# A two-layer transformer tower on one core: row maxima moved into their own layer's units, the stretch between iterations reordered, six heads' output projection moved into the attention

## The reference

```python
h = x @ W + pe                                            # 29 -> 128 channels
h = h + attn0(ln(h))      # group norm, 8 heads of 64, softmax over 1024 keys, wo, + its own input
h = h + ffn0(ln(h))       # tril(W1), gelu, tril(W2) over the 128 channels
h = h + attn1(ln(h))      # 8 heads of 16, softmax over 1024 keys, Wo
h = h + switch(ln(h))     # 16 experts, top 1, capacity 1.2, scaled by the route's probability
```

## Time and profile before

| | |
|---|---|
| median of 3 runs | 8374.74 us (8361.47 to 8421.3) |
| profiled execution, its own time | 8371.84 us |
| its span, first to last instruction | 8370.1 us |
| mean granted TensorE clock | 0.833 of full speed |
| busy PE / DVE / ACT / POOL | 88% / 60% / 38% / 21% |

### The profile page before, as it was taken

The page is one execution under the profiler, slowest core; times in us unless marked ns, Lnnn a source line. Parts: engine busy times, 40 slices in busy tenths (PEclk is TensorE's granted clock), DMA queues, the critical chain, the costliest instruction groups (busy, mean ns, idle before and its releaser), DMA issues.

```text
span 8370.1 us, 124378 instructions
## 1 busy us (share of the span) xinstructions
PE 7405.4 (88%) x39399; PEld 4297.5 (51%) x39399; DVE 5002.4 (60%) x11545; ACT 3213.9 (38%) x6291; POOL 1774.3 (21%) x1623
## 2 busy tenths in 40 slices
PE   6798998989989899898988989899898998989987
PEld 4555555545545455454555545555554555545532
DVE  5664665656666565565656656566565665656554
ACT  3343443433434343343433434334343443434431
POOL 2322222222222222222221222222222221222200
PEclk8887897988988878798887888879788787888866
DMA  2220211111121110211102111111111111111000
GB/s 63 47 47 20 49 32 40 39 43 36 26 49 39 33 39 23 49 39 33 39 22 52 37 43 39 29 43 29 43 39 41 31 32 43 38 40 39 22 24 7
DMA packets 89184, 308.91 MB, mean 37 GB/s; under 512 B 23942, under 2 KB 30022, under 8 KB 78278
## 3 DMA queue, kind: packets, MB, share of 16 engines
q1 hardware_dynamic: 88518, 300.53, 15.6%
HBM read 49.33 MB, written 41.94 MB: 11 GB/s over the span
## 4 chain that ended last, share of the span: by engine, by line
issue 63%; POOL 17%; PE 14%; DVE 4%; DMA 1%; POOLq 0%; SPq 0%; ACT 0%; DVEq 0%; ACTq 0%
POOL pr_lo L456 9%; POOL on L1183 3%; PE bank L776 3%; PE bank L749 2%; POOL on L1175 2%; PE bank L735 2%; PE bank L792 1%; PE bank L806 1%; PE bank L793 1%; PE bank L774 1%; DVE hm L1448 1%; DMA stacks<-parts 1%; DVE mxh L1458 1%; POOL h L1153 1%; PE bank L816 1%
## 5 line engine op out<-in xcount | busy, mean ns | idle before, releaser
L1458 DVE TENSOR_REDUCE mxh<-bank 128x1 f32<-128x512 f32 x4096 | 2761.3, 689 | 2300.8 <-PE bank L749 2275.4
L1029 ACT ACTIVATE pr<-bank 128x512 f32<-128x512 f32 x4096 | 2400.1, 598 | 3343.0 <-PE bank L776 3276.2
L749 PE MATMUL bank<-stacks 128*128 128x512 f32 (+1 forms) x4096 | 2036.1, 508 | 403.3 <-DVE mxh L1458 369.6
L776 PE MATMUL bank<-stacks 65*128 65x512 f32 (+1 forms) x4096 | 1929.2, 482 | 5.7 <-ACT pr L1029 5.7
L749 PEld LDWEIGHTS bank<-stacks 128*128 128x128 f32 (+1 forms) x4096 | 862.8, 214 | 1088.0 <-DVE mxh L1458 791.0
L456 POOL TENSOR_TENSOR pr_lo<-pr 128x1024 bf16<-128x1024 f32 x496 | 940.1, 1895 | 1933.7 <-ACT pr L1029 1933.7
L792 PE MATMUL bank<-v,pr 128*128 128x129 bf16 x8192 | 1308.1, 251 | 7.5 <-DVE pr_lo L456 5.1
L793 PE MATMUL bank<-v,pr_lo 128*128 128x129 bf16 x7936 | 1272.2, 251 | 0.0
L776 PEld LDWEIGHTS bank<-stacks 65*128 65x128 f32 (+1 forms) x4096 | 839.5, 210 | 767.7 <-issue 609.6
L774 PE MATMUL bank<-stacks 128*128 128x512 f32 x2048 | 1049.8, 513 | 47.0 <-issue 40.8
L792 PEld LDWEIGHTS bank<-v,pr 128*128 128x128 bf16 x8192 | 904.1, 113 | 357.1 <-issue 338.7
(11 more groups left out here) (180 smaller groups left out, 5209.8 us busy)
## 6 DMA issues: line engine op xcount, KB each, us to landing
stacks<-parts SPq DMA_DIRECT2D x384, 512.0 KB, 6.7
parts_d<-pr SPq DMA_DIRECT2D x16, 2048.0 KB, 6.5
stacks<-parts_d SPq DMA_DIRECT2D x224, 128.0 KB
stacks<-parts_d SPq DMA_DIRECT2D x224, 64.0 KB
stacks<-mrow SPq DMA_DIRECT2D x512, 2.0 KB
out<-hm SPq DMA_DIRECT2D x16, 512.0 KB, 2.7
stacks<-pr SPq DMA_DIRECT2D x32, 128.0 KB
stacks<-pr SPq DMA_DIRECT2D x32, 64.0 KB
```

The costliest lines, as they stand in the source:

```text
L749: mm(maxb[k % 2][:, :], qs[:, t * P:(t + 1) * P], ks[:, g * HALF:(g + 1) * HALF], start=True, stop=True).then_inc(max_filled.sem, 1)
L776: mm(bank[:, :], k_stack(layer, head)[0:last, kk], q_stack(layer, head)[0:last, q], start=(layer == 1), stop=True).then_inc(score_filled.s ...
L1029: act.activation(pr[:, at % 2, kt, :], score[k % 2][:, :], ACT.Exp, scale=SCALES[layer]).then_inc(exp_done.sem, 1)
L1458: dve.tensor_reduce(mxh[:, layer, n // 2, n % 2:n % 2 + 1], maxb[k % 2][:, :], AX_X, ALU.max)\
```

## The change

1. `tile_step` and `row_step` are shifted by two steps. A layer 0 unit's eight steps now hold only layer 0's tiles and a layer 1 unit's only layer 1's; before, the steps 6 and 7 of each unit held tiles of the other layer. Early tiles fall from 18 to 16.
2. `values1` is one piece of eight matmuls at step 3.
3. The expert blocks stand at s = 8m+5 of other units: seven layer 0 units (m = 12, 14, 20, 22, 24, 26, 28) and nine layer 1 units. Before there were four and twelve. Projections stand one slot earlier.
4. The output projection of heads 0 to 5 (`attn0a`) runs at the slots 244 and 247 of the attention; DVE adds it to `h0`. `serial` keeps the last two heads'.
5. `serial` has another order on every engine: layer norm 1 is applied before the old image's attention result is added; the first feed-forward matmul comes ahead of the next image's turn; the next image's group norm and heads come ahead of layer norm 2; POOL's two residual sums come last; the early maxima of layer 0 stand between two halves of the next image's values.

```diff
     if layer == 0:
-        return n - 18 if n < 8 else n - 10
-    return n - 10 if n < 8 else n - 2
+        return n - 16 if n < 8 else n - 8
+    return n - 8 if n < 8 else n
...
-    return (((-8, 8), (0, 16))[layer] if kind in BOTH else (-4, 4))[g]
+    return (((-6, 10), (2, 18))[layer] if kind in BOTH else (-4, 4))[g]
...
+def partial_slots(kind):
+
+    return {"first": {"attn0a.0": 113, "attn0a.1": 118}, "final": {}}.get(kind, {"attn0a.0": 244, "attn0a.1": 247})
...
-        first = [8 * m + 2 for m in sorted([*range(7, 31, 2), 14, 18, 22, 26])]
+        first = [8 * m + 5 for m in (7, 11, 12, 13, 14, 15, 19, 20, 21, 22, 23, 24, 26, 27, 28, 29)]
...
+                for g in range(2):
+                    yield partial_slots(seg.kind)[f"attn0a.{g}"]
+                    heads_out(seg, f"attn0a.{g}", g, range(NCH - 1))
...
-            def values1(seg, at, j):
+            def values1(seg, at):
                 _, u = units_of(seg.kind)[at]
                 n = o_place(seg.kind, 1, u)
-                te.wait_ge(exp_done.sem, exp_done.at(seg, 8 * at + 4 * j + 4))
-                if j == 0:
-                    te.wait_ge(o_drained.sem, o_drained.at(seg, n - 1))
+                te.wait_ge(exp_done.sem, exp_done.at(seg, 8 * at + 8))
+                te.wait_ge(o_drained.sem, o_drained.at(seg, n - 1))
```

In `serial`, on DVE:

```diff
+                if seg.l0:
+                    norm_apply(seg.l0, 1, h)
+                if seg.nxt:
+                    await_drained(dve, seg, "h0", "h1")
+                    norm_stats(seg, 0, h0)
                 if seg.l1:
                     dve.wait_ge(hm_copied.sem, hm_copied.at(seg.l1, 1))
                     for g in range(2):
                         add_result(seg, f"attn1.{g}", g, hm, hm)
...
+                if seg.nxt:
+                    embed_var(seg, "")
+                    embed_norm(seg, seg.nxt)
+                    embed_heads(seg, "", seg.nxt)
+                if seg.l0:
                     await_drained(dve, seg, "ffn_o0", "ffn_o1")
                     norm_stats(seg, 2, h)
```

In `serial`, on POOL:

```diff
                 if seg.nxt:
+                    rstd(seg, seg.nxt, 4)
+                if seg.l0:
+                    rstd(seg, seg.l0, 2)
+                if seg.nxt:
                     residual0(seg, seg.nxt)
-                if seg.l0:
-                    rstd(seg, seg.l0, 2)
-                if seg.nxt:
-                    rstd(seg, seg.nxt, 4)
```

More of the change, by code:

```diff
@@ L176, in glue_plan @@
     for name in SERIAL_NAMES:
-        wanted = kind != "first" if name in OLD_NAMES else kind not in ("penult", "final") if name in EMBED_NAMES \
+        after = next_kind(kind)
+        wanted = after is not None and int(name[1]) in layers_of(after) and early_row(after, int(name[1])) if name[0] == "M" \
+            else kind != "first" if name in OLD_NAMES else kind not in ("penult", "final") if name in EMBED_NAMES \
             else kind != "final"
         uses += [name] if wanted else []
-    after = next_kind(kind)
-    for layer in layers_of(after) if after else ():
-        uses += [f"M{layer}.0.0"] if early_row(after, layer) else []
     if kind == "final":
@@ L689, in done_heads, with heads_out @@
                         heads_turn(seg, c, g)
+                for g in range(2):
+                    yield partial_slots(seg.kind)[f"attn0a.{g}"]
+                    heads_out(seg, f"attn0a.{g}", g, range(NCH - 1))
+            def heads_out(seg, name, g, chunks):
+                bank, filled = use(seg, name, *(f"oT0.{c}.{g}" for c in chunks))
+                for j in range(4):
+                    t = 4 * g + j
+                    for c in chunks:
+                        last = mm(bank[:, j * P:(j + 1) * P], heads_T(c)[:, t * P:(t + 1) * P], wo_sb[:, c, :],
+                                  start=(c == chunks[0]), stop=(c == chunks[-1]))
+                last.then_inc(filled, 1)
             def old_turn(seg):
@@ L841, in serial @@
                 at = len(units_of(seg.kind)) - 1
-                for j in range(4 if seg.kind == "first" else 2):
-                    values(seg, at, j)
+                after = next_kind(seg.kind)
+                for j in range(4):
+                    if seg.kind == "first" or j < 2:
+                        values(seg, at, j)
                 if seg.l0:
@@ L852, in serial @@
                     for g in range(2):
[L853 to L859 removed]
+                        heads_out(seg, f"attn0.{g}", g, (3,))
                 if seg.nxt:
@@ L875, in serial @@
                 if seg.nxt:
+                    for g in range(2):
+                        z_turn(seg, seg.nxt, 0, g)
                     embed_group(seg, "", seg.nxt, 0)
@@ L902, in serial @@
                 if seg.nxt:
-                    embed_values(seg, "")
+                    embed_values(seg, "", range(4))
+                    early(seg, "next", after, 0)
+                    embed_values(seg, "", range(4, T))
                 if seg.l0:
-                    early(seg, "next", next_kind(seg.kind))
-                if seg.l0:
+                    early(seg, "next", after, 1)
                     await_drained(te, seg, "v1.0", "v1.1")
@@ L925, in segment @@
                     embed_values(seg, "a.")
-                    early(seg, "now", "first")
+                    early(seg, "now", "first", 0)
                     await_drained(te, seg, "a.v0.6", "a.v0.7")
@@ L1098, in serial @@
                 if seg.nxt:
-                    embed_values(seg, "")
-                after = next_kind(seg.kind)
-                for layer in layers_of(after) if after else ():
-                    if early_row(after, layer):
-                        max_rows(seg, f"M{layer}.0.0", seg.following(layer), layer, 0, 0)
+                    embed_values(seg, "", range(4))
+                    max_rows(seg, "M0.0.0", seg.nxt, 0, 0, 0)
+                    embed_values(seg, "", range(4, T))
+                if seg.l0 and early_row(after, 1):
+                    max_rows(seg, "M1.0.0", seg.l0, 1, 0, 0)
             def segment(seg):
@@ L1228, in serial @@
                 if seg.nxt:
[L1229 removed]
+                    residual0(seg, seg.nxt)
             def segment(seg):
@@ L1562, in serial @@
                 if seg.nxt:
-                    embed_values(seg, "", seg.nxt)
+                    embed_values(seg, "", seg.nxt, range(4))
+                    early(seg, "next", after, 0)
+                    embed_values(seg, "", seg.nxt, range(4, T))
                 if seg.l0:
-                    early(seg, "next", next_kind(seg.kind))
+                    early(seg, "next", after, 1)
             def segment(seg):
@@ L1578, in segment @@
                     embed_values(seg, "a.", seg.l0)
-                    early(seg, "now", "first")
-                beside = [Beside(more_heads(seg))] if seg.l0 else []
+                    early(seg, "now", "first", 0)
+                beside = [Beside(more_heads(seg)), Beside(partial(seg))] if seg.l0 else []
                 if seg.sw:
```

105 lines of the change are left out of this document (46 added, 59 removed).

## The result

The changed kernel takes **9098.2 us** (median of 4 runs, 9088.7 to 9128.4), the kernel before 8382.4 in the same measurement: ratio **1.085**, 95% interval 1.081 to 1.090. The forecast was 8420, its range ended at 8620. Slower was the side with the largest chance (0.36), but the size lies far outside. The profiled execution lasts 9086.9 us, 716.8 more than before.

The account below looks back on a forecast made before the run. Attention bound by PE's work in layer 0 units and a three-engine chain starting layer 1. Terms -16 + 18 + 3 + 4 - 4 = +5, times 14 is +70, second segment -20: 8371.8 + 50 = 8422, forecast 8420 us, range 8190 to 8620.

Parts of the forecast that it names:

- the blocks' places: Expert blocks in the attention: matmul cost plus stalls rise from 44 to 62 us, +18 an iteration, bounds 0 and +26.
- The stalls: Multiply-adds ahead of the low half lengthen seven layer 1 starts by 2.1 us; ahead of max tiles, nine stalls of 2.1.
- 6.3 was asked for: Sign of being right: layer 0 units with a block take 6.3 us or more from last score to first values, not 4.27.
- The clock: PE clock falls at layer 1 starts (2.2 us each) and new layer 0 stalls: +3 an iteration, bounds -20 and +14.
- after a wait of 0.69 in weak work: Argument for the slower rival: at the start of layer 1 the clock now falls after PE waits 0.69 us.
- The second rival: Multiply-adds ahead of layer 0 units' first tiles drop the clock in all nine places: +24 an iteration, about 8690, chance 0.23.
- Tiles and values1, -16 an iteration: In attention units, own-layer tiles and one-piece values1 save 1.2 us a pair over 13 pairs: -16, bounds -8 and -20.
- a bound of -8: Smallest saving from tiles and values1 in the attention, if DVE is late wherever PE is early: -8 us an iteration.
- Six heads, +4: 48 projection matmuls return on PE in the last pair, 2.7 us at each of two slots, partly covering a wait: +4.
- Serial, -4: Serial stretch: layer 1's q comes 2 us earlier, early tiles save 0.8, one collision costs 1.9: -4, bounds -10 and +2.
- The collision: In serial, POOL's residual sums start as DVE applies layer norm 2: eight operations take 4.07, not 2.14; one stop, +1.9.

Follow-up runs that it names:

- The added matmuls: Changed kernel with two more block-size matmuls, results unread, at steps 2 and 3 of layer 1 units of pairs 6, 10, 12, 14: 8975.9 us, ratio 1.070.
- the early matmuls: Changed kernel with the blocks' matmuls on PE at 8m + 2 and 8m + 3, multiply-adds on DVE left at step 7: 8977.4 us, ratio 1.067.
- the run with the wait: Changed kernel with old places of blocks and projections, and POOL's two residual sums held until layer norm 2 is applied: 8318.9 us, ratio 0.993.
- 8247: Kernel before with values1 in one piece, six heads in the attention, and POOL's layer norm 1 sum held until the next image's norm: 8246.7 us, ratio 0.984.

## Why the prediction was wrong, and where it was right

**The sum against the runs.** Per iteration it said +18 and +3 for the blocks' places and their clock, -12 for tiles, values1 and six heads together, -4 for serial: +5. Measured are +50.3 (attention 422.8 with the old slots of blocks and projections, 473.1 with the new), +1.7 (421.1 and 422.8) and +1.5: 53.5. So of the 48.5 that it missed, 29 are the first item, 14 the second, 5.5 the third.

**The stalls were right.** The sum had 2.1 us of growth in front of the low half and a stall of 2.1 behind a layer 1 block. Measured: last score to first values 6.55 (6.3 was asked for), and a wait of 1.95 for DVE's max tile at step 2; over the nine layer 0 units behind a block, step 2 takes 2.1 to 3.3 us, 0.8 to 1.0 in neighbours without. The place, the engine, the queue and the duration are as the list of DVE told.

**The clock was the step that failed.** It stood at +3 an iteration. The placement costs 50.3. Of these 18 were predicted for the two stalls and the blocks' matmuls; the other 32 come with 84 us more of low clock (108.7 and 192.4). The step priced a fall at 2.2 us, "values at 1.2 GHz", as if the clock then came back. In the four units below it came back early only where full-size matmuls followed the first values. Before, a block stood at steps 2 and 3 of every layer 1 unit from pair 3 to pair 14, right behind the first values; the working counted it at steps 5 and 6 as the same work. With it gone, the clock stays low through most of a unit of 21 to 23 us in four pairs of each iteration. These four are 27 us longer than with the old slots, 8 of them the predicted stall, which leaves 19 for the clock; the seven falls in layer 0 units add 1.5 each (step 3 takes 4.2 to 4.4, 3.7 in pair 15, and not 2.75): 29 of the 32. That split is worked out from lengths; shown by edits are the 121 and 122 us of the early and the added matmuls. The added matmuls, the early matmuls, and pair 12 with and without a block show it from three sides.

The prediction also misread its own row. It has the clock fall "after a wait of 0.69 in weak work". That wait ends at 3191.34, and the records of the kernel before have the clock low from 3189.48: it fell while PE went from one narrow matmul to the next, and their durations grew there:

```profile
3188.47 0.39 PE L776 MATMUL bank<-stacks 49*128 49x512 f32 x1
...
3189.60 0.63 PE L749 MATMUL bank<-stacks 48*128 48x512 f32 x1
3190.03 0.63 PE L776 MATMUL bank<-stacks 49*128 49x512 f32 x1
3191.34 0.79 PE L749 MATMUL bank<-stacks 48*128 48x512 f32 x1 [0.69 <-DVE mxh L1458]
```

So the clock had to be priced by the kind of work on PE as well as by its waits.

**The second rival had the side but not the mechanism.** "Every stall drops the clock" gave 8690 (its terms add up to 8698). The clock did fall in seven of the nine layer 0 units behind a block, at some 1.5 us each as priced. It misses the other 400 us mostly for the same reason as the forecast.

**Tiles and values1, -16 an iteration, failed in the loops.** values1 alone gave -5.6 there, more than its share of 4; the tiles alone +2.1. A layer 0 unit without a block did get shorter (9.5 to 8.7, 0.8; the working's own terms for it add up to about 0.7). But the next unit can't start earlier: in the kernel before, last score to first values took 3.97 us in pair 10 of one iteration, with the tiles moved and the blocks' old places 4.08. The chain over ACT and DVE takes back what PE saves in front of it. The prediction named this ("if DVE is late wherever PE is early") as a bound of -8, and even that bound was too good. In the second segment -16.5 stand beside the -20 predicted, but this is in part luck: the tiles alone gave -18.4 and values1 alone -17.0, where the working has 0.9 and 0.3 a pair, 14 and 5, and together they don't add up. Each time the low clock fell by 31 to 37 us, and at half the speed such a stretch costs up to half its length (an estimate), 16 to 19. The final segment was put down as unchanged and got 34 us shorter, 31 with values1 alone. Here too the gain isn't where the working looked: with values1 alone the steps 2 and 3, where it stands, take 5.36 in place of 5.47 us (means of its units 2 to 13), the steps 5 and 6 3.69 in place of 5.19, and the low clock of the segment falls from 194 to 119 us. What in the one piece keeps the clock up isn't shown.

**Six heads, +4:** +2.9 in the last pair, when its effect on the clock of the next unit is counted, against 3.5 to 5.2 saved in serial. Over a whole iteration the two pairs of runs disagree: 9.6 gained on the changed kernel with its blocks at step 2, 4.2 lost on the kernel before, and in both the low clock of other units moves too. So its worth stays open. The first segment pays for it (209.8 to 217.0 with this and values1, 209.9 with values1 alone), which the sum left out.

**Serial, -4, came out at +1.5.** The collision was named but counted once. Both residual sums stop DVE: 6.23 = 2.14 + 4.09, 2.2 more than the 4.07 counted. The prediction set the rule of the Trainium skill (SBUF — State Buffer, "Who interferes with whom") beside it: the shared port pair goes to whoever starts first, for the whole instruction, so two sums stop DVE twice. The trace agrees with the rule, and the run with the wait shows its price, 3.8 us an iteration. The other 3 us are missing even with that wait, for which the sum would be -6 and the run shows -2.9: the new order brings nothing that the old one with six heads hasn't (87.9 and 87.3).

**What stays open.** In the layer 1 units behind a stall, the low stretch lasts about 7 us in odd pairs and 17 in even ones. Both hold the same kinds of work; at full clock (kernel before) steps 4 and 5 take 0.57 and 1.57 in pair 10, 0.34 and 1.34 in pair 11. The traces show what differs. An even pair's layer 1 unit computes max tiles of its own head, whose operand lies on the same 64 partitions as that of the score (`stacks1[64 * (head % 2):...]`), and the tile starts behind the score; an odd pair's computes those of the next head, on the other 64, and in six of eight steps score and tile start together. Pair 10, then pair 11, in the changed kernel:

```profile
3997.12 0.79 PE L792 MATMUL bank<-stacks 49*128 49x512 f32 x1
3997.71 0.63 PE L766 MATMUL bank<-stacks 48*128 48x512 f32 x1
...
4032.52 0.79 PE L792 MATMUL bank<-stacks 49*128 49x512 f32 x1
4032.52 0.79 PE L766 MATMUL bank<-stacks 48*128 48x512 f32 x1
```

That this decides when the clock comes back was not tested. Nor was a version with own-layer tiles tuned to the end: its best run, 8319, is behind 8247.

## What to carry to other kernels

Price a stall by what PE does after it, too. In four units of each iteration the clock stayed low for 17 us where no dense matmuls followed the first values and for 7 to 10 where they did, so dense side work belongs right behind the weak stretch, and moving it away is a cost of its own. On an engine with a list in order, put side work behind the operation that another engine waits for, never in front of it, even if a step of slack seems to lie there. And if two changes shorten the same stretch in front of a fixed chain, count the gain once, or not at all.

## What the runs showed of the hardware

- Adding 112 full-size matmuls to the program made it 122 us faster, at an unchanged stall (6.55 us) and a mean granted clock of 0.813 in place of 0.791.
- The clock stayed low for 16.8 us in units in which PE was hardly ever idle (18.96 of 22.56 us busy, the other 3.60 in one wait), and in the kernel before it fell with PE busy (3189.48). So a full row of PE's busy time doesn't mean that the clock is up, and only the column of the granted clock tells.
- Two POOL sums of 2.34 us each, back to back, stretch eight DVE operations from 2.14 to 6.23 us, one stop for each sum; with POOL held back the serial stretch was 3.8 us shorter.
- values1 in one piece, alone, raised the granted clock of the final segment from 0.62 to 0.73, with the same matmuls.
- Two narrow matmuls (49 and 48 rows) started in the same instant where their operands lay on different halves of the partitions, and one behind the other where they lay on the same half (4032.52; 3997.12 and 3997.71).
